# Layer-norm factors applied behind the projection, and ScalarE shares a multiplication with GpSimd, in a Fourier-attention block followed by a recurrent layer

## The chip, the core and the metric

One core of one Trainium2 chip runs the kernel. The core has five engines with their own instruction queues: TensorE (PE in the profile; its weight loads are PEld), VectorE (DVE), ScalarE (ACT), GpSimd (POOL) and SyncE (SP), which here only issues DMAs. They meet through semaphores. The metric is the device time of one launch in microseconds (us).

## The reference, cut to what matters

The input is `x`, 4 x 32 tokens of 128 x 128 float32. A Fourier attention block with a mixer is added to it; the result `t`, seen as rows of 128 values, goes through a second layer norm, a projection `W`, a batch norm and a sigmoid recurrence with `V`.

```python
x = x + conv_ref(ln_c(x), ...)            # attention, mixer, instance norms
t = to_tokens(x)                          # rows of 128 values
t = t + ffn_ref(ln_t(t), W, V, gamma, beta)

def ln_t(v, eps=1e-5):                    # the second LayerNorm
    m = mean(v, -1); s = var(v, -1)
    return (v - m) / sqrt(s + eps)

def ffn_ref(x, W, V, gamma, beta):
    Wx = einsum('bti,hi->bth', x, W)
    mean, var = moments of Wx over all rows, one pair per h
    Wx = (Wx - mean) * rsqrt(var + 1e-5) * gamma + beta
    # y_t = sigmoid(Wx_t + y_(t-1) @ V.T), scanned over t
```

The last step of the mixer in `conv_ref` adds, for every token, a multiple `bet` of the mixer's first output to the attention's result and to the second Fourier product.

## The kernel before, in words

All data stay in three SBUF buffers of 128 x 16384 float32: BIG1, BIG2 and BIG3. Tokens are handled in groups of four (G4 = 32 groups, counted by g) and in chunks of sixteen tokens (XC = 8 chunks, counted by c; a chunk is four groups). The order of the work on each engine is written out by hand: each engine has a loop over steps `i`, and fixed lags say which group a part of the step works on. Waits on semaphores tie the loops of the engines together.

The stage that the change touches is the last loop before the recurrence. Its parts, by engine:

- GpSimd (L612 to L623): for each step `bm1`, m1 of group i times `bet` (L618, in place in BIG1, 512 columns), then `xm`, a0 of group i-1 plus that product (L623). Ahead of steps 7, 11, 15, ... it waits until the layer-norm factors of chunk (i-3)//4 - 1 are there (`ln2_coef`, L615), so its work comes in bursts of four steps. Behind the loop it adds `g0` to the 32 groups of a0 (L632), 24 of them (G0_EARLY) before it waits for the recurrence's first state.
- TensorE (L893 to L913): `pair` multiplies the second Fourier product for two groups into banks 4 to 7; then it transposes four tokens of the normalised m1 of group i-7 (L906), and multiplies the transposed group i-9 by `w_t` (L913) into bank 2 or 3.
- VectorE (L1468 to L1490): adds the Fourier product to a0 of group i-1 (`x1`, L1474), takes the row statistics of its four tokens (four bn_stats, recorded at L1193), at every fourth group works out the chunk's moments (L1202 to L1206, the last of which asks for a root), normalises the fourth token of every other group (L1483), takes statistics of W's product of group i-12 for the batch norm (L1488), and at steps 5, 9, 13, ... turns the root into the factors `ln_r` and `ln_b` (L1212, L1213, which increments `ln2_coef`).
- ScalarE (L1110 to L1131): the root (L977), the normalisation of four or three tokens of group i-6 from a0 into m1, with scale and bias per row (L1118), the copy of the transposed group from PSUM to `ln_w` (`move_lnw`, recorded at L390, "SML<-PS"), and the copy of W's product from PSUM to BIG3 (L1130).

When the batch norm's statistics are complete (`bn`), VectorE aggregates them (L1495), asks for one more root (L1175) and computes the factors; TensorE meanwhile runs WARM = 4 dummy matmuls of 512 columns (L919) and then the recurrence, 24 steps in four groups, on TensorE, VectorE (L1505) and ScalarE (L1139 to L1152). Results are transposed back and added to a0 (L1548), stored by SyncE, and a judge (L1529 to L1539) decides whether the recurrence has converged.

Helpers record many operations under one line: matmuls at L644, transposes at L648, copies at L390, bn_stats at L1193.

## Time and profile before

| what | us |
|---|---|
| median of three runs | 474.27 |
| lowest, highest | 474.26, 479.56 |
| the profiled execution, its own time | 473.51 |
| its span in the trace | 471.4 |
| PE busy | 361.6 |
| DVE busy | 345.7 |
| ACT busy | 263.7 |
| POOL busy | 234.0 |

The span is the stretch from the first to the last recorded instruction of the profiled execution; the 2.1 us between it and the execution's own time lie outside the trace. A busy time is a sum over the whole span, so it does not say which engine limits a stage. Stretches are given in us from the span's start.

### The profile page before, as it was taken

What the parts mean: (1) busy time and instruction counts of PE and PEld (TensorE: products, weight loads), DVE (VectorE), ACT (ScalarE), POOL (GpSimd) and SP (SyncE); (2) the same over time, 40 slices, a digit from 0 to 9 for tenths busy, and PEclk for the clock granted to TensorE, in tenths of its full rate; (3) what the DMA queues carried; (4) which work ended last, traced back from release to release, by engine and by line L of the source; (5) the groups of instructions that cost most, each with busy time, mean ns of one, the idle gap of its engine ahead of it and who ended that gap; (6) DMA issues with size and microseconds to landing.
All of it is one profiled execution on the core that took longest, in us unless ns stands there. A gap on an engine that the chain in (4) does not pass through costs nothing.

```text
span 471.4 us, 7104 instructions
## 1 busy us (share of the span) xinstructions
PE 361.6 (77%) x2409; PEld 279.3 (59%) x2409; DVE 345.7 (73%) x946; ACT 263.7 (56%) x530; POOL 234.0 (50%) x276
## 2 busy tenths in 40 slices
PE   0169999998948998899961956867777488999970
PEld 0169986884528998788861843433334135766970
DVE  3698512888969573999948477777778837899992
ACT  0778762620135874556511305989888797899200
POOL 1399960000027957999210567777666985300000
PEclk9979999999997999999995885998898979999995
DMA  8999896789140002999977000000000000000698
GB/s 214 264 295 309 234 296 180 163 233 424 81 179 2 1 1 24 118 129 143 126 93 87 2 0 0 3 0 0 0 1 1 0 0 1 0 3 0 188 287 243
DMA packets 60696, 50.97 MB, mean 108 GB/s; under 512 B 4513, under 2 KB 54097, under 8 KB 59633
## 3 DMA queue, kind: packets, MB, share of 16 engines
q1 hardware_dynamic: 40928, 41.79, 30.4%
q0 software_dynamic: 16512, 8.39, 14.6%
q10 hardware_dynamic: 3216, 0.30, 0.6%
q8 instruction: 21, 0.34, 0.3%
q14 instruction: 19, 0.15, 0.1%
HBM read 30.45 MB, written 16.88 MB: 100 GB/s over the span
## 4 chain that ended last, share of the span: by engine, by line
PE 34%; DVE 29%; POOL 19%; ACT 6%; issue 5%; ACTq 3%; DMA 1%; SPq 0%; POOLq 0%; DVEq 0%
PE PS L644 31%; POOL BIG L583 8%; DVE BIG L1300 4%; DVE SML L1193 4%; DVE BIG L1474 3%; POOL BIG L623 3%; DVE BIG L1548 2%; POOL BIG L618 2%; PE PS L648 2%; DVE SML L1488 2%; POOL BIG L602 2%; ACTq L1000 2%; ACT BIG L1118 2%; ACT SML L390 2%; DMA BIG<-xn_rows 1%
## 5 line engine op out<-in xcount | busy, mean ns | idle before, releaser
L644 PE MATMUL PS<-CST,BIG 128*128 128x128 f32 (+6 forms) x994 | 129.5, 324 | 22.5 <-ACT BIG L1014 9.4
L644 PEld LDWEIGHTS PS<-CST,BIG 128*128 128x128 f32 (+1 forms) x994 | 114.4, 202 | 41.9 <-issue 11.9
L648 PE MATMUL PS<-CST,BIG 128*128 128x128 f32 (+1 forms) x326 | 54.6, 314 | 47.7 <-ACT SML L390 22.8
L648 PEld LDWEIGHTS PS<-CST,BIG 128*128 128x128 f32 (+1 forms) x326 | 43.9, 194 | 71.8 <-issue 52.3
L596 POOL COPY BIG<-BIG 128x512 f32<-128x512 f32 x24 | 30.5, 1328 | 74.4 <-DMA BIG<-xn_rows 71.3
L1193 DVE BATCH_NORM_STATS2 SML<-BIG 128x6 f32<-128x128 f32 x256 | 53.4, 279 | 6.3 <-DMA BIG<-in_x 5.0
L618 POOL TENSOR_TENSOR BIG<-BIG,SML 128x512 f32<-128x512 f32 x32 | 33.2, 1038 | 45.9 <-DVE SML L1213 28.0
L644 PE MATMUL PS<-BIG 128*128 128x128 f32 (+2 forms) x450 | 53.5, 368 | 2.6 <-DVE BIG L1300 2.1
L390 ACT ACTIVATE BIG<-PS 128x512 f32<-128x512 f32 (+3 forms) x59 | 33.2, 572 | 33.5 <-PE PS L644 26.5
L644 PE MATMUL PS<-BIG,SML 128*128 128x256 f32 (+4 forms) x230 | 48.9, 415 | 0.0
L644 PEld LDWEIGHTS PS<-BIG 128*128 128x128 f32 (+2 forms) x450 | 40.6, 168 | 13.1 <-issue 8.2
L1118 ACT ACTIVATE BIG<-BIG,SML 128x128 f32<-128x128 f32 x112 | 46.0, 482 | 3.8 <-DVE SML L1213 3.8
L1505 DVE SCALAR_TENSOR_TENSOR PS<-BIG,SML,PS 128x256 f32<-128x256 f32 x92 | 41.2, 489 | 3.6 <-PE PS L644 3.5
L602 POOL TENSOR_TENSOR BIG<-BIG,SML 128x512 f32<-128x512 f32 x32 | 39.5, 2476 | 7.0 <-ACT BIG L1083 7.0
L644 PE MATMUL PS<-SML 128*128 128x512 f32 (+2 forms) x74 | 41.1, 640 | 0.6 <-ACT BIG L1130 0.6
L623 POOL TENSOR_TENSOR BIG<-BIG 128x512 f32<-128x512 f32 x32 | 40.5, 1267 | 0.0
L644 PEld LDWEIGHTS PS<-BIG,SML 128*128 128x128 f32 (+1 forms) x230 | 31.1, 178 | 15.2 <-ACT BIG L1152 3.5
L583 POOL TENSOR_SCALAR BIG<-BIG,SML 128x128 f32<-128x128 f32 x84 | 36.8, 446 | 0.0
L1152 ACT ACTIVATE BIG<-PS,SML 128x256 f32<-128x256 f32 x80 | 35.5, 474 | 0.4
L632 POOL TENSOR_TENSOR BIG<-BIG,SML 128x512 f32<-128x512 f32 x32 | 32.0, 1037 | 6.9 <-ACT BIG L1139 6.9
L1474 DVE TENSOR_TENSOR BIG<-BIG,PS 128x512 f32<-128x512 f32 x32 | 21.7, 678 | 18.5 <-POOL BIG L623 16.9
L390 ACT ACTIVATE SML<-PS 128x512 f32<-128x512 f32 x32 | 34.4, 1075 | 0.0
(209 smaller groups left out, 516.0 us busy)
## 6 DMA issues: line engine op xcount, KB each, us to landing
xn_rows<-BIG SPq DMA_DIRECT2D x8, 1024.0 KB, 7.7
BIG<-xn_rows SPq DMA_DIRECT2D x8, 1024.0 KB, 9.3
BIG<-in_x POOLq DMA_DIRECT2D x8, 1024.0 KB, 11.0
out_x<-BIG SPq DMA_DIRECT2D x32, 256.0 KB, 3.6
BIG<-wy_rows SPq DMA_DIRECT2D x16, 192.0 KB, 5.4
BIG<-BIG SPq DMA_DIRECT2D x16, 192.0 KB, 4.0
BIG<-in_L_conv_mixer_w SPq DMA_DIRECT2D x2, 544.0 KB, 7.4
CST<-in_const SPq DMA_DIRECT2D x1, 547.5 KB, 8.7
```

Source lines behind the costliest of these rows:

```text
L390: return e.activation(o, i, ACT.Copy) if e is scalar_engine else e.tensor_copy(o, i)
L583: last = pool.tensor_scalar(x_h[:, n, :], x_h[:, n, :], ln_r[:, n:n + 1], ln_b[:, n:n + 1], ALU.mult, ALU.add)
L602: pool.tensor_tensor(m1[:, v, :], a0[:, v, :], kap[:, v].unsqueeze(2).to_broadcast([128, 4, W]), ALU.mult).then_inc(S("ka0"), 1)
L618: pool.tensor_tensor(m1[:, v, :], m1[:, v, :], bet[:, v].unsqueeze(2).to_broadcast([128, 4, W]), ALU.mult).then_inc(S("bm1"), 1)
L623: pool.tensor_tensor(a0[:, v, :], a0[:, v, :], m1[:, v, :], ALU.add).then_inc(S("xm"), 1)
L644: return pe.matmul(o, l, rhs, start=start, stop=stop, **k)
L648: return pe.matmul(o, i, ident[0:n, 0:n], is_transpose=True, start=True, stop=True)
L1118: last = act.activation(m1[:, n, :], a0[:, n, :], ACT.Identity, scale=ln_r[:, n:n + 1], bias=ln_b[:, n:n + 1])
L1152: act.activation(at(y_s, g, i * 2 + (j0 + dj)), sums(g, dj), ACT.Sigmoid, bias=s("bb")).then_inc(S("state"), 1)
L1193: last = dve.bn_stats(ln_st[:, c % 2, row, :], src[:, XR * c + row, :])
L1474: TT(v, v, halves(4 + g % 4), ALU.add).then_inc(S("x1"), 1)
L1505: STT(sums(b, dj), wx_step[:, b, :, bass.ds(j, 1), :], s("bs"), sums(b, dj), ALU.mult, ALU.add).then_inc(S("vy_wx"), 1)
```

## The change

Three things are changed, and constants with them.

First, the layer norm is no longer applied ahead of the transposes. The row mean of W is taken off W at the start (`w_centred`, on VectorE), so a row's own mean drops out of the product. TensorE transposes a0 itself and multiplies by the centred W. The factor 1/sqrt(var+eps) of each row is then multiplied into W's product: VectorE reads the product from PSUM and the factors from SBUF, writes BIG3 and sums the result in the same instruction (`STT ... accum_out`, in place of bn_stats). ScalarE squares the result with an offset and sums that (`Square`, with an accumulator output), in place of the copy. The row factors lie one per partition, and are wanted along the free dimension in all partitions: SyncE writes the 128 x 16 factors of a chunk to DRAM (8 KB), waits, and reads them back broadcast to 128 partitions (1 MB) into the chunk's part of BIG1.

Second, GpSimd multiplies two of each four tokens by `bet`, and ScalarE the two others (`bm1_act`, two copies of 128 columns with a scale per row), six groups ahead.

Third, GpSimd's bursts are released by the chunk's moments (`root_of`) and not by its factors; the transposed group is copied to `ln_w` in another order of its columns; the last four products have banks of their own; and 11 of the `g0` additions, not 24, come before the wait for the first state, behind all moments.

```diff
-LAG_LN, LAG_TR, LAG_MV, LAG_W, LAG_WX, LAG_BN = 6, 7, 8, 9, 10, 12
+LAG_TR, LAG_MV, LAG_W, LAG_WX, LAG_SQ = 6, 7, 8, 9, 10
-G0_EARLY, WARM = 24, 4
+G0_EARLY, WARM = 11, 4
+BM_ACT, LEAD = 2, 6
+ROOTS_1 = XC + 6
...
+        row_scale = BIG1[:, :].rearrange("d (c h t) -> d c h t", c=XC, t=XR)
+        def w_bank(g):
+            return 2 + g % 2 if g < G4 - 4 else 8 - G4 + g
+        def scale_of(g):
+            return row_scale[:, g // 4, :, 4 * (g % 4):4 * (g % 4) + 4]
...
-            return copy(e, ln_w[:, n % 2].rearrange("w (h t) -> w t h", t=4),
-                        bank(n % 2).rearrange("w (t h) -> w t h", t=4))
+            return copy(e, ln_w[:, n % 2].rearrange("w (h t) -> w h t", t=4),
+                        bank(n % 2).rearrange("w (t h) -> w h t", t=4))
... SyncE
+            for c in range(XC):
+                sp.wait_ge(S("ln2_coef"), c + 1)
+                sp.dma_start(rs_rows[c], ln_r[:, XR * c:XR * c + XR]).then_inc(S("rs_out"), 16)
+                sp.wait_ge(S("rs_out"), 16 * (c + 1))
+                sp.dma_start(row_scale[:, c].rearrange("d h t -> d (h t)"),
+                             flat(rs_rows[c]).to_broadcast([128, H * XR])).then_inc(S("rs_in"), 16)
... GpSimd
-                    pool.wait_ge(S("ln2_coef"), (i - 3) // 4)
+                    pool.wait_ge(S("root_of"), ROOTS_1 + (i - 3) // 4)
                 if i < G4:
-                    v = slice(4 * i, 4 * i + 4)
+                    v = slice(4 * i + BM_ACT, 4 * i + 4)
...
+                    pool.wait_ge(S("bm1_act"), i)
...
+            pool.wait_ge(S("root_of"), ROOTS_1 + XC)
             for g in range(G4):
-                pool.wait_ge(S("ln2_act"), g + 1)
-                pool.wait_ge(S("ln2_dve"), LN2_DVE[g])
+                pool.wait_ge(S("lnw_filled"), g + 1)
... TensorE
+            pe.wait_ge(S("w_centred"), 1)
...
+                    pe.wait_ge(S("x1"), 2 * (g // 2) + 2)
-                        last = tr(PS[:, g % 2, 128 * j:128 * j + 128], m1[:, 4 * g + j, :])
+                        last = tr(PS[:, g % 2, 128 * j:128 * j + 128], a0[:, 4 * g + j, :])
...
-                    mm(bank(2 + g % 2), w_t, ln_w[:, g % 2]).then_inc(S("wx_filled"), 1)
+                    mm(bank(w_bank(g)), w_t, ln_w[:, g % 2]).then_inc(S("wx_filled"), 1)
... ScalarE
+            def bm1_act(g):
+                for n in range(4 * g, 4 * g + BM_ACT):
+                    last = act.activation(m1[:, n, :], m1[:, n, :], ACT.Copy, scale=bet[:, n:n + 1])
+                last.then_inc(S("bm1_act"), 1)
             empty(act, "zt2", 0, 8, move_zt(4))
+            act.wait_ge(S("ka0"), G4)
+            act.wait_ge(S("bet"), 1)
+            for g in range(LEAD):
+                bm1_act(g)
             empty(act, "ta2", 0, 8, move_ta(ta2, 0))
-            for i in range(G4 + LAG_WX):
+            for i in range(G4 + LAG_SQ):
...
-                    for n in range(4 * g, 4 * g + LN2_ACT[g % 2]):
-                        last = act.activation(m1[:, n, :], a0[:, n, :], ACT.Identity,
-                                              scale=ln_r[:, n:n + 1], bias=ln_b[:, n:n + 1])
...
+                if i + LEAD < G4:
+                    bm1_act(i + LEAD)
+                g = i - LAG_SQ
                 if g >= 0:
-                    act.wait_ge(S("wx_filled"), g + 1)
-                    act.activation(wx(g), bank(2 + g % 2).rearrange("d (h t) -> d h t", t=4),
-                                   ACT.Copy).then_inc(S("wx"), 1)
+                    act.wait_ge(S("pivot"), 1)
+                    act.wait_ge(S("wx"), g + 1)
+                    act.activation(scale_of(g), wx(g), ACT.Square, bias=s("npiv"),
+                                   accum_out=bn_sq[:, g:g + 1]).then_inc(S("bn"), 1)
... VectorE
+            dve.wait_ge(S("ffn_in"), 16 * 4)
+            link(dve.tensor_reduce(s("wm"), w_t, AX.X, ALU.add))
+            link(TS(s("wm"), s("wm"), 1.0 / W, None, ALU.mult))
+            TS(w_t, w_t, s("wm"), None, ALU.subtract).then_inc(S("w_centred"), 1)
...
-                if 0 <= g < G4 and LN2_ACT[g % 2] < 4:
-                    for n in range(4 * g + LN2_ACT[g % 2], 4 * g + 4):
-                        last = TS(m1[:, n, :], a0[:, n, :], ln_r[:, n:n + 1], ln_b[:, n:n + 1], ALU.mult, ALU.add)
...
+                    dve.reciprocal(rs, rs).then_inc(S("ln2_coef"), 1)
+                g = i - LAG_WX
                 if g >= 0:
-                    dve.wait_ge(S("wx"), g + 1)
-                    dve.bn_stats(bn_st[:, g, :], wx(g)).then_inc(S("bn"), 1)
-                if i % 4 == 1 and 0 <= i // 4 - 1 < XC:
-                    ln_coefs(i // 4 - 1, "ln2_coef")
+                    dve.wait_ge(S("wx_filled"), g + 1)
+                    if g % 4 == 0:
+                        dve.wait_ge(S("rs_in"), 16 * (g // 4 + 1))
+                    STT(wx(g), bank(w_bank(g)).rearrange("d (h t) -> d h t", t=4), 1.0, scale_of(g),
+                        ALU.mult, ALU.mult, accum_out=bn_sum[:, g:g + 1]).then_inc(S("wx"), 1)
...
-            link(dve.bn_aggr(sc[:, 60:62], bn_st.rearrange("d g c -> d (g c)")))
+            dve.tensor_reduce(sc[:, 60:61], bn_sum, AX.X, ALU.add)
+            link(dve.tensor_reduce(sc[:, 61:62], bn_sq, AX.X, ALU.add))
+            # four small operations turn the sums into mean and variance
```

## Rows read from the trace of the kernel before

**Rows 1.** The chain that ended last, shares of the span, from the page.
```profile
PE 34%; DVE 29%; POOL 19%; ACT 6%; issue 5%; ACTq 3%; DMA 1%; SPq 0%; POOLq 0%; DVEq 0%
```
**Rows 2.** A stretch: from:to, length, busy PE PEld DVE ACT POOL, PEclk, DMA, GB/s.
```profile
274.80:391.10 116.30, 77.77 (x312) 39.82 (x308) 87.22 (x258) 91.12 (x184) 84.93 (x79) 0.84 0.00 1
```
**Rows 3.** Timeline of POOL, 334 to 348: start, duration, line, idle before, releaser.
```profile
334.22 1.04 POOL L618 TENSOR_TENSOR BIG<-BIG,SML 128x512 f32<-128x512 f32 x1 [4.08 <-DVE SML L1213]
335.22 1.27 POOL L623 TENSOR_TENSOR BIG<-BIG 128x512 f32<-128x512 f32 x1
...
347.24 1.04 POOL L618 TENSOR_TENSOR BIG<-BIG,SML 128x512 f32<-128x512 f32 x1 [4.08 <-DVE SML L1213]
```
**Rows 4.** Timeline of DVE in the same stretch.
```profile
338.74 0.69 DVE L1474 TENSOR_TENSOR BIG<-BIG,PS 128x512 f32<-128x512 f32 x1 [2.38 <-POOL BIG L623]
...
343.15 0.22 DVE L1202 TENSOR_TENSOR SML<-SML 128x32 f32<-128x32 f32 x1
...
343.78 0.68 DVE L1488 BATCH_NORM_STATS2 SML<-BIG 128x6 f32<-128x512 f32 x1
344.38 0.67 DVE L1474 TENSOR_TENSOR BIG<-BIG,PS 128x512 f32<-128x512 f32 x1
345.08 0.87 DVE L1193 BATCH_NORM_STATS2 SML<-BIG 128x6 f32<-128x128 f32 x4
345.87 0.33 DVE L1483 TENSOR_SCALAR BIG<-BIG,SML 128x128 f32<-128x128 f32 x1
...
346.99 0.17 DVE L1213 SCALAR_TENSOR_TENSOR SML<-SML 128x16 f32<-128x16 f32 x1
```
**Rows 5.** Groups by line and shape, whole span: busy, mean ns, idle before.
```profile
L1083 ACT ACTIVATE BIG<-PS 128x512 f32<-128x512 f32 x32 | 18.7, 595 | 9.0 <-PE PS L644 8.6
L1051 ACT ACTIVATION_READ_ACCUMULATOR BIG<-BIG 128x1 f32 x1 | 0.2, 187 | 0.0
L1447 DVE SCALAR_TENSOR_TENSOR BIG<-BIG,SML 128x512 f32<-128x512 f32 x2 | 2.2, 1158 | 0.0
```
**Rows 6.** Timeline of ACT: four normalisations in one piece.
```profile
334.18 1.65 ACT L1118 ACTIVATE BIG<-BIG,SML 128x128 f32<-128x128 f32 x4 [0.47 <-DVE SML L1213]
```
**Rows 7.** DMA issues: KB each, us from issue to landing.
```profile
BIG<-in_x POOLq DMA_DIRECT2D x8, 1024.0 KB, 11.0
BIG<-in_L_conv_mixer_w SPq DMA_DIRECT2D x2, 544.0 KB, 7.4
wy_rows<-BIG SPq DMA_DIRECT2D x1, 96.0 KB, 6.2
BIG<-in_L_conv_key_w ACTq DMA_DIRECT2D x1, 18.0 KB, 2.5
```
**Rows 8.** Timeline of PE: product and pair at half clock, transposes and product at full.
```profile
292.24 1.92 PE L644 MATMUL PS<-SML 128*128 128x512 f32 x2
294.09 2.08 PE L644 MATMUL PS<-CST,BIG 64*128 64x256 f32 x8
...
341.12 0.63 PE L648 MATMUL PS<-CST,BIG 128*128 128x128 f32 x4
341.58 1.02 PE L644 MATMUL PS<-SML 128*128 128x512 f32 x2
```
**Rows 9.** Timelines, end of the loop: DVE in the last moments and at the last root.
```profile
368.74 1.07 DVE L1203 TENSOR_TENSOR SML<-SML 128x16 f32<-128x16 f32 x1
392.14 0.15 DVE L1175 TENSOR_SCALAR SML<-SML 128x1 f32<-128x1 f32 x1
```
**Rows 10.** Timeline of PE: the recurrence's first products.
```profile
394.86 12.71 PE L644 MATMUL PS<-BIG,SML 128*128 128x256 f32 x56
```
**Rows 11.** Stretches around an idle TensorE; columns as in rows 2.
```profile
250.00:254.00 4.00, 0.00 (x0) 0.00 (x0) 3.68 (x12) 0.00 (x0) 0.00 (x0) 0.50 1.26 158
258.00:262.00 4.00, 4.00 (x20) 3.31 (x20) 2.48 (x9) 1.18 (x2) 0.00 (x0) 0.50 0.00 0
262.50:264.50 2.00, 1.70 (x16) 1.43 (x14) 1.25 (x4) 1.02 (x2) 0.22 (x1) 1.00 0.00 0
```

More of the change, by code:

```diff
@@ L311, in metaformer @@
         ln_tmp = SML[:, 2496:2624].rearrange("p (k v) -> p k v", v=16)
-        bn_st = SML[:, 1984:2176].rearrange("p (g c) -> p g c", c=6)
+        bn_sum = SML[:, 1984:1984 + G4]
+        bn_sq = SML[:, 2016:2016 + G4]
         scn = {}
@@ L334, in metaformer @@
         wy_rows = nc.dram_tensor("wy_rows", [NH, 3 * MW * MH], F32).ap()
+        rs_rows = nc.dram_tensor("rs_rows", [XC, H, XR], F32).ap()
         xn_tok = nc.dram_tensor("xn_rows", [NT, H, W], F32).ap()
@@ L350, in metaformer @@
         modes_ps = PS[:, 4:6, :].rearrange("t a n -> t (a n)")
-        LN2_DVE = np.cumsum([LN2_ACT[g % 2] < 4 for g in range(G4)]).tolist()
         P2_N = [min(P2_T, NT - P2_T * g) for g in range((NT + P2_T - 1) // P2_T)]
@@ L1465, in _ @@
             empty(dve, "ta2", 0, 8, move_ta(ta2, 0))
-            for i in range(G4 + LAG_BN):
+            assert roots[0] == ROOTS_1
+            for i in range(G4 + LAG_WX):
                 g = i - 1
@@ L1479, in _ @@
                         ln_rows(g // 4, a0, four_at(g % 4))
-                g = i - LAG_LN
-                if 0 <= g < G4 and LN2_ACT[g % 2] < 4:
-                    for n in range(4 * g + LN2_ACT[g % 2], 4 * g + 4):
-                        last = TS(m1[:, n, :], a0[:, n, :], ln_r[:, n:n + 1], ln_b[:, n:n + 1], ALU.mult, ALU.add)
-                    last.then_inc(S("ln2_dve"), 1)
-                g = i - LAG_BN
-                if g >= 0:
-                    dve.wait_ge(S("wx"), g + 1)
-                    dve.bn_stats(bn_st[:, g, :], wx(g)).then_inc(S("bn"), 1)
-                if i % 4 == 1 and 0 <= i // 4 - 1 < XC:
-                    ln_coefs(i // 4 - 1, "ln2_coef")
+                if i % 4 == 1 and 0 <= i // 4 - 1 < XC:
+                    c = i // 4 - 1
+                    roots[0] += 1
+                    dve.wait_ge(S("root"), roots[0])
+                    rs = ln_r[:, XR * c:XR * c + XR]
+                    dve.reciprocal(rs, rs).then_inc(S("ln2_coef"), 1)
+                g = i - LAG_WX
+                if g >= 0:
+                    dve.wait_ge(S("wx_filled"), g + 1)
[3 more added lines that the diff above has]
+                        ALU.mult, ALU.mult, accum_out=bn_sum[:, g:g + 1]).then_inc(S("wx"), 1)
+                    if g == 0:
+                        dve.wait_ge(S("wx"), 1)
+                        TS(s("npiv"), bn_sum[:, 0:1], -1.0 / (4 * H), None, ALU.mult).then_inc(S("pivot"), 1)
             dve.memset(start_b[:, 0, 0:NT:TB], 0.0)
             dve.wait_ge(S("bn"), G4)
-            link(dve.bn_aggr(sc[:, 60:62], bn_st.rearrange("d g c -> d (g c)")))
+            dve.tensor_reduce(sc[:, 60:61], bn_sum, AX.X, ALU.add)
+            link(dve.tensor_reduce(sc[:, 61:62], bn_sq, AX.X, ALU.add))
+            link(TS(sc[:, 60:61], sc[:, 60:61], 1.0 / (NT * H), None, ALU.mult))
+            link(TT(s("x0"), sc[:, 60:61], s("npiv"), ALU.add))
+            link(TT(s("x0"), s("x0"), s("x0"), ALU.mult))
+            link(STT(sc[:, 61:62], sc[:, 61:62], 1.0 / (NT * H), s("x0"), ALU.mult, ALU.subtract))
             inv_root(s("bs"), sc[:, 61:62], EPS, s("gamma"))
```

16 lines of the change are left out of this document (5 added, 11 removed).

## The prediction

> **What bounds the kernel now.** I read the chain of waits first. TensorE, VectorE and GpSimd share it [rows 1], so no engine bounds the whole kernel and a stage has to be read by itself. Then the busy times of the stage that the change rewrites, from the first addition of the second Fourier product to the complete batch-norm sums, 274.8 to 391.1 us: in 116.3 us no engine is busy for more than 91, DMA is idle, and the mean granted clock is 0.84 [rows 2]. So a loop of waits sets the pace, and the timelines show it. GpSimd starts a burst of four steps at 334.22 and the next at 347.24, 13.02 us apart, and stood idle for 4.08 us ahead of each, released by L1213, the layer-norm factors on VectorE [rows 3]. VectorE stood idle for 2.38 us until the burst's second addition, worked to the chunk's moments at 343.15 (done by 343.78), and reached L1213 at 346.99 only behind a statistics pass, an addition, four row statistics and a normalisation that its loop puts in between [rows 4]. GpSimd 4.5, VectorE 5.0, then 3.4 between moments and factors: that is the 13.0. At the end of the loop the last moments meet GpSimd's g0 additions, and an operation with two small SBUF inputs takes 1.07 us [rows 9] where its group of four took 0.63 [rows 4].
>
> **The change part by part.** All sums are against the profiled execution (span 471.4, time 473.5; the median shown is 0.8 above that).
>
> *GpSimd.* Its burst is released by the moments, 3.4 us earlier, and L618 covers half the columns: by its 1.04 us about 0.55, against 1.27 for the addition [rows 3]. Less the overlap of neighbours a burst takes 4 x (0.55 + 1.23) = 7.1 us, its half that VectorE wants first 3.6. VectorE now has a longer way to its next moments than that, so GpSimd leaves the path.
>
> *VectorE.* Per step it keeps the addition, 0.70 start to start, and four row statistics, 0.79 [rows 4]. It loses the statistics pass (0.60) and half a normalisation, and gets a product of 512 columns from PSUM and SBUF with a sum. The trace has no such form. The nearest rows are L1488, 0.60 start to start over the same view [rows 4], and, on the dear side, L1447, an operation of the same kind with both tensors in SBUF, 1.16 [rows 5]; reading out the sum costs 0 to 0.19, ScalarE's price for it [rows 5]. Its one SBUF tensor and PSUM tensor are as in L1474, which runs undisturbed, so I take 0.75, ends 0.60 and 1.35. A step is then 0.70 + 0.79 + 0.75 = 2.24. Four make 9.0; with moments 0.75 and the reciprocal 0.25 a chunk takes 10.0.
>
> The Trainium skill (Vector Engine (DVE) Microarchitecture Reference, Points that are easy to get wrong) says that this kind with two SBUF sources that aren't bf16 runs at half speed. The 1.16 us of L1447 agrees. By that rule one source in PSUM escapes it; were the rule to hold for it too, the sum would be that of the first rival below.
>
> *ScalarE.* Per step it loses 3.5 normalisations and a copy. It keeps the move to `ln_w`, now in the order of columns that L1083 has: 0.60 [rows 5]. It gets two copies of 128 columns, 1.65 / 4 = 0.41 each [rows 6], so 0.82, and a square of 512 columns with a sum: 0.60 as L1083, and 0.19 to read out [rows 5]. That is 2.2, with the root some 9.1 a chunk, under VectorE but close. For two engines that hand work to each other at 90% I add 0.2: 10.2 us a chunk.
>
> *TensorE* does the same work. At full clock a group's transposes take 0.46 to the next start and a product about 0.87, a pair half of 2.08: 4 x 1.33 + 2 x 1.04 = 7.4 us a chunk; at half clock 14.9 [rows 8]. Under 10.2, so it idles little.
>
> *SyncE and the DMA.* The path from factors to broadcast is a new wait: store 8 KB, wait, load 1 MB. The small store I take at 2.5, the load of 18 KB, with 6.2 (96 KB to DRAM under load) as upper end. For the load of 1 MB I take 5.5, between 2.5 and 7.4 (544 KB broadcast, beside other traffic), upper end 11.0 [rows 7]. With 0.3 for the two starts L = 8.3, between 5.3 and 17.5. No other transfer runs then. VectorE waits for it four steps behind the factors, 10.2 us, so in the loop it is hidden, until L passes 10.2; then two chunks take L + 10 us. At the last chunk nothing covers it.
>
> The Trainium skill (DMA: Bandwidth & Descriptors, Anatomy of one DMA and Specifications) gives about 2.0 us plus bytes over 436 GB/s, an estimate of 2.0 and 4.4 for the two; it also says that pieces under 512 B are read, changed and written, which speaks against the 64 B pieces of this store. No row here has that store, and by the first rule the end would come 1.6 us earlier than I say.
>
> *The start.* ScalarE does the first 12 half-multiplications ahead of its moves of `ta2`: 4.9 us, of which most hides behind TensorE filling the other banks. I charge 0.7. Centring W adds three small operations to VectorE early, while it waits for other engines: nothing, and at most 0.8 if that cover were gone. Squares and sums in place of bn_stats change the end by 0.2.
>
> *The clock.* At the end TensorE finishes its products about 8 us before the sums are complete. In the rows, an idle TensorE is at 0.50, the lower level, 1.2 GHz (250 to 254); still at 0.50 through four busy microseconds (258 to 262), and at 1.00, 2.4 GHz, from 262.5 [rows 11]. So the dummy matmuls start low. Eight halves of 0.92 at the low level [rows 8]: 4.5 us low, the rest at full, 6.2 in all with the small matmul ahead, against 3.8 now. The recurrence starts 2.4 later after the sums. A low clock at the first products costs me 1.0 more.
>
> *The sum.* First addition 275.5. Four steps of 1.49 and moments: 282.2. The next step and factors of chunk 0: 284.0. Steps 6 to 8 wait for GpSimd (3.6 us behind 282.2) and meet its burst in the moments; factors of chunk 1 at 291.9; the row factors of chunk 0 land at 284.0 + 8.3 = 292.3. From there 0.75 + 3 x 2.24 + 0.75 + 1.5 + 0.3: factors of chunk 2 at 302.3. Four chunks of 10.2: 343.1. The last has no further addition: 343.1 + 10.2 - 1.5 = 351.8. Landing 8.3 later, 360.1. Four products 3.0, the last square 0.8: 363.9. Small operations 1.2: root asked at 365.1, against 392.14 [rows 9]. The recurrence starts at 363.9 + 6.2 = 370.1 against 394.86 [rows 10]. That is 24.8 earlier, less 1.0 for the clock at the start: 23.8. GpSimd's 21 remaining g0 additions take 22 us of a recurrence of 44, hidden. 473.5 - 23.8 = 449.7; against the median 450.5. I predict 450.
>
> **The rivals.**
> 1. *Dear operations.* If the product with its sum takes 1.16 to 1.2, a chunk is 12.0 and the six chunks and the tail give back 1.8 x 6 = 11: 461. For it: L1447 [rows 5]. Against: L1474 and L1488, both 0.6 to 0.7 with this view or a PSUM source.
> 2. *The transfer paces the loop.* At L = 12 two chunks take 22 and not 20.4, three times, and the tail is 3.7 longer: 450 + 5 + 4 = 459. For it: 7.4 us for half the bytes, broadcast [rows 7]. Against: that one ran beside others.
> 3. *The transfer makes it slower.* The same mechanism, further out: the end moves 4 us for each 1 us of L beyond 10.2 (three pairs of chunks and the tail). To eat up 24 us it takes L = 16, to be slower by 2% 18. With 6.2 + 11.0, the dearest rows of either kind [rows 7], L is 17.5: 450 + 2 + 4 x 7.3 = 481. Against: both rows were taken with the DMA engines full, and here they are empty [rows 2].
> 4. *TensorE at half clock.* If it falls as it does now in this stage (0.84 on average), products take twice as long for some microseconds. All of the loop at 14.9 a chunk would give 450 + 28 = 478, no change. For it: 0.50 after idle stretches [rows 11]. Against: at 7.4 of 10.2 busy and with busy stretches that bring the clock back, only pieces of it.
> 5. *Cheap operations.* Product 0.60, L 6.7: 0.7 x 6 + 1.6: 444.
> 6. *The change doesn't do what it says*: the release at the moments brings nothing because additions wait for ScalarE's halves. They are six groups ahead, so I give it nothing of its own; it is part of 4.
>
> **How the numbers follow.** Forecast 0.55, rivals 0.15, 0.13, 0.04, 0.06, 0.07. Two per cent of 474.27 is 9.5, about what a measurement of this kernel tells from no change: faster is under 464.8. The forecast, 1, 5 and nearly all of 2 lie there: 0.89. Rival 4 and the edge of 2 give 0.07 within 2%, rival 3 gives 0.04. The range 442 to 464 holds the forecast (446 to 455), most of 1, 2 and 5, and leaves out 3 and 4.
>
> **What would show it.** GpSimd's bursts 10 to 10.5 us apart, released by L1206's successor and not by the factors, and no idle VectorE ahead of the addition. The product's row near 0.7 us; a read-out row behind it or none. `ln_w` moves of 0.6. VectorE idle for 5 to 6 us once, ahead of product 28, released by the broadcast. TensorE at 0.50 when the dummy matmuls start. Wrong would be: bursts over 12 us apart, an idle VectorE at every fourth product (the transfer), or TensorE over 90% busy in the loop.

## The result and the profile after

The changed kernel takes 438.99 us (median of four runs, 437.13 to 440.65) against 474.34 us before on the same chip: a ratio of 0.9229, 95% interval 0.9188 to 0.9269. The forecast was 450 with 442 to 464: the direction was right, and the gain, 35 us where 24 were forecast, was larger than the range allowed.

| | before | after |
|---|---|---|
| profiled execution, its own time | 473.51 | 440.65 |
| its span | 471.4 | 438.7 |
| first addition of the loop | 274.81 | 277.37 |
| moments of the eighth chunk done | 371.78 | 347.31 |
| root of the batch norm asked | 392.14 | 359.01 |
| recurrence starts | 394.86 | 361.71 |

From first addition to root the stage went from 117.3 to 81.6 us. Of that, 27.0 lies between the first addition and the last moments (the loop), and 8.7 behind them, where ScalarE used to pace the last groups: before the change VectorE's statistics waited up to 2.23 us for its copies there.

```profile
383.12 0.69 DVE L1488 BATCH_NORM_STATS2 SML<-BIG 128x6 f32<-128x512 f32 x1 [2.23 <-ACT BIG L1130]
```

The stage after the change in one row, to be held against [rows 2] (same columns):

```profile
277.30:357.90 80.60, 65.51 (x312) 35.85 (x309) 73.40 (x266) 56.09 (x149) 58.01 (x63) 0.96 0.30 106
319.00:349.00 30.00, 24.55 (x117) 12.99 (x116) 28.85 (x107) 20.94 (x53) 19.15 (x21) 1.00 0.29 107
```

In the middle of the loop (second row) VectorE is busy for 28.85 of 30 us. Before, no engine was the bound, the waits between them were; now one is, at 96%. TensorE runs at 1.00 there, and the DMA engines, idle before, are busy for 29%.

GpSimd's timeline, as [rows 3]:

```profile
319.56 0.61 POOL L635 TENSOR_TENSOR BIG<-BIG,SML 128x256 f32<-128x256 f32 x1 [2.02 <-DVE SML L1232]
320.13 1.28 POOL L642 TENSOR_TENSOR BIG<-BIG 128x512 f32<-128x512 f32 x1
...
328.83 0.61 POOL L635 TENSOR_TENSOR BIG<-BIG,SML 128x256 f32<-128x256 f32 x1 [2.01 <-DVE SML L1232]
```

The bursts are 9.27 us apart (13.02 before), released by the moments. VectorE over one of its steps and over the moments, as [rows 4]; L1505 is the addition, L1219 the row statistics, L1522 the product:

```profile
304.38 0.87 DVE L1219 BATCH_NORM_STATS2 SML<-BIG 128x6 f32<-128x128 f32 x4
305.17 0.67 DVE L1522 SCALAR_TENSOR_TENSOR BIG<-PS,BIG 128x512 f32<-128x512 f32 x1
305.77 0.08 DVE L1522 DVE_READ_ACCUMULATOR BIG<-PS,BIG 128x1 f32 x1
305.77 0.68 DVE L1505 TENSOR_TENSOR BIG<-BIG,PS 128x512 f32<-128x512 f32 x1
306.48 0.87 DVE L1219 BATCH_NORM_STATS2 SML<-BIG 128x6 f32<-128x128 f32 x4
...
309.49 0.21 DVE L1228 TENSOR_TENSOR SML<-SML 128x32 f32<-128x32 f32 x1
...
310.12 0.68 DVE L1522 SCALAR_TENSOR_TENSOR BIG<-PS,BIG 128x512 f32<-128x512 f32 x1
...
312.24 0.23 DVE L1516 RECIPROCAL SML<-SML 128x16 f32<-128x16 f32 x1
312.39 0.62 DVE L1522 SCALAR_TENSOR_TENSOR BIG<-PS,BIG 128x512 f32<-128x512 f32 x1
```

From start to start the product takes 0.60, the addition 0.71 and the statistics 0.79: 2.10 a step. (The operation behind the addition reads what it wrote, the one behind the product does not; whether that is the 0.11 between them was not tested.) The read-out of the sum has a row of its own, 0.08 us, that starts at the same moment as the next addition. With moments and reciprocal a chunk takes 9.28 us, and from 289 to 348 us no row shows VectorE idle. ScalarE over one step:

```profile
319.73 0.58 ACT L400 ACTIVATE SML<-PS 128x512 f32<-128x512 f32 x1
320.21 0.68 ACT L1129 ACTIVATE BIG<-BIG,SML 128x128 f32<-128x128 f32 x2
320.79 0.71 ACT L1156 ACTIVATE BIG<-BIG,SML 128x512 f32<-128x512 f32 x1
321.40 0.19 ACT L1156 ACTIVATION_READ_ACCUMULATOR BIG<-BIG,SML 128x1 f32 x1
321.50 0.58 ACT L400 ACTIVATE SML<-PS 128x512 f32<-128x512 f32 x1
```

The step takes 1.77 us; 2.2 were forecast. The new transfer, from the page's DMA issues, and the end of the loop on VectorE and TensorE:

```profile
BIG<-rs_rows SPq DMA_DIRECT2D x8, 1024.0 KB, 4.6
```
```profile
350.50 0.69 DVE L1522 SCALAR_TENSOR_TENSOR BIG<-PS,BIG 128x512 f32<-128x512 f32 x1 [0.60 <-PE PS L663]
...
354.17 0.69 DVE L1522 SCALAR_TENSOR_TENSOR BIG<-PS,BIG 128x512 f32<-128x512 f32 x1 [1.67 <-DMA BIG<-rs_rows]
...
359.01 0.15 DVE L1201 TENSOR_SCALAR SML<-SML 128x1 f32<-128x1 f32 x1
```
```profile
357.95 3.92 PE L663 MATMUL PS<-CST,SML 128*128 128x1 f32 x10 [1.78 <-ACT BIG L1156]
```

Behind the last moments VectorE is no longer full: its products come 1.30 us apart, each waiting for TensorE's product, which waits for ScalarE's copy. SyncE issues the store at 348.12 and the load at 349.52, and it lands at 354.17: 6.08 us from the factors (348.09), of which VectorE stood idle for 1.67. TensorE had been idle for 1.78 us when the dummy matmuls began, and they ran at full clock, 3.9 us.

### The profile page after: what moved, and what is told of

It reads as the page before. It is cut to its first block, busy times and chain, and to the rows that moved or that the text cites. A ratio compares the mean times of both kernels' runs of the same rounds, so it can differ in the third digit from the quotient of the medians.

```text
span 438.7 us, 7163 instructions
## 1 busy us (share of the span) xinstructions
PE 352.2 (80%) x2409; PEld 278.3 (63%) x2409; DVE 332.1 (76%) x963; ACT 233.8 (53%) x514; POOL 220.5 (50%) x276
## 4 chain that ended last, share of the span: by engine, by line
PE 37%; DVE 30%; POOL 15%; issue 8%; ACT 4%; ACTq 3%; DMA 2%; SPq 0%; DVEq 0%; POOLq 0%
PE PS L663 34%; POOL BIG L600 8%; DVE BIG L1330 5%; DVE SML L1219 4%; DVE BIG L1505 4%; DVE BIG L1522 3%; PE PS L667 3%; DVE BIG L1589 3%; POOL BIG L619 2%; ACTq L1020 2%; DMA BIG<-xn_rows 2%; DVE BIG L1422 1%; DVE BIG L1418 1%; POOL BIG L642 1%; POOL BIG L635 1%
## 5 line engine op out<-in xcount | busy, mean ns | idle before, releaser
L663 PE MATMUL PS<-CST,BIG 128*128 128x128 f32 (+6 forms) x994 | 127.2, 318 | 21.1 <-ACT BIG L1034 8.0
L667 PE MATMUL PS<-CST,BIG 128*128 128x128 f32 (+1 forms) x326 | 51.0, 300 | 15.2 <-DVE BIG L1477 14.3
L663 PE MATMUL PS<-BIG 128*128 128x128 f32 (+2 forms) x450 | 55.8, 375 | 2.6 <-DVE BIG L1330 2.1
L1219 DVE BATCH_NORM_STATS2 SML<-BIG 128x6 f32<-128x128 f32 x256 | 53.4, 279 | 5.8 <-DMA BIG<-in_x 4.5
L663 PEld LDWEIGHTS PS<-BIG 128*128 128x128 f32 (+2 forms) x450 | 42.8, 175 | 13.2 <-issue 8.4
L619 POOL TENSOR_TENSOR BIG<-BIG,SML 128x512 f32<-128x512 f32 x32 | 39.5, 2476 | 7.0 <-ACT BIG L1103 7.0
L663 PE MATMUL PS<-SML 128*128 128x512 f32 (+2 forms) x74 | 35.2, 560 | 9.3 <-DVE BIG L1522 8.0
L651 POOL TENSOR_TENSOR BIG<-BIG,SML 128x512 f32<-128x512 f32 x32 | 32.0, 1042 | 9.3 <-issue 6.3
L635 POOL TENSOR_TENSOR BIG<-BIG,SML 128x256 f32<-128x256 f32 x32 | 19.6, 612 | 33.8 <-DVE SML L1490 17.5
L663 PE MATMUL PS<-SML,BIG 128*128 128x128 f32 (+1 forms) x264 | 33.1, 287 | 1.0 <-DVE SML L1376 1.0
L663 PEld LDWEIGHTS PS<-SML,BIG 128*128 128x128 f32 (+1 forms) x264 | 32.1, 202 | 2.0 <-DVE SML L1376 1.3
L1113 ACT ACTIVATE BIG<-BIG,SML 128x512 f32<-128x512 f32 x32 | 22.8, 721 | 19.0 <-DVE BIG L1418 19.0
```

Of the source, the lines that this page charges most:

```text
L619: pool.tensor_tensor(m1[:, v, :], a0[:, v, :], kap[:, v].unsqueeze(2).to_broadcast([128, 4, W]), ALU.mult).then_inc(S("ka0"), 1)
L635: pool.tensor_tensor(m1[:, v, :], m1[:, v, :], bet[:, v].unsqueeze(2).to_broadcast([128, 4 - BM_ACT, W]), ALU.mult).then_inc(S("bm1"), 1)
L651: pool.tensor_tensor(a0[:, v, :], a0[:, v, :], g0[:, v].unsqueeze(2).to_broadcast([128, 4, W]), ALU.add).then_inc(S("x1_g0"), 1)
L663: return pe.matmul(o, l, rhs, start=start, stop=stop, **k)
L667: return pe.matmul(o, i, ident[0:n, 0:n], is_transpose=True, start=True, stop=True)
L1219: last = dve.bn_stats(ln_st[:, c % 2, row, :], src[:, XR * c + row, :])
```

## The experiments

In all of them "chunk" is the distance between the moments of neighbouring chunks in the profiled execution. The runs were made in three sets, each with the kernel before in it; its medians there were 474.9, 475.6 and 476.5 us, and each ratio is against its own set.

**1. After, with GpSimd released by the factors again.**

```diff
-                    pool.wait_ge(S("root_of"), ROOTS_1 + (i - 3) // 4)
+                    pool.wait_ge(S("ln2_coef"), (i - 3) // 4)
```

> The changed kernel, with GpSimd's bursts again released by the chunk's factors and not by its moments. Theory A (in the new loop VectorE's own work, 9.28 us a chunk, is the pace, and the early release only keeps GpSimd out of its way): the factors come 2.3 us behind the moments, the half of the burst that VectorE wants first takes 3.65 more, and VectorE wants it 4.85 behind the moments, so it waits 1.1 us a chunk: chunks of 10.4 us, 6 to 8 us in all, some 446. Rival B (the release was the whole gain, the rest only moved work about): chunks go back to about 13 us, some 460. Rival C (the release is worth nothing once the operations are cheaper): 439.

447.47 us, ratio 0.9452 (0.9367 to 0.9536); chunks of 10.47 us.

```profile
317.56 0.69 DVE L1505 TENSOR_TENSOR BIG<-BIG,PS 128x512 f32<-128x512 f32 x1 [1.10 <-POOL BIG L642]
```

VectorE's wait for GpSimd is back, 1.10 us once a chunk (the next is at 328.03, 10.47 later). The release is worth 1.2 us a chunk here, 8.5 in all by the medians. Not all of that is the wait: the ten dummy matmuls took 5.62 us and not 3.92, for the granted clock fell within a microsecond or so of their start (0.71 in 364 to 365, 0.50 in 365 to 367). That is theory A; B (460) and C (439) are out.

**2. Before, with only the release at the moments.**

```diff
-                    pool.wait_ge(S("ln2_coef"), (i - 3) // 4)
+                    pool.wait_ge(S("root_of"), XC + 6 + (i - 3) // 4)
```

> The kernel before, with nothing changed but that GpSimd's bursts are released by the moments. Theory A: the loop of 13.02 us was GpSimd 4.5, VectorE 5.0 and 3.4 between moments and factors; without the 3.4 the next limit is ScalarE, which idles 1.64 us of the 13.02, so chunks of 11.4 and a total 8 to 11 us shorter than before, some 464 to 466. Rival B (the release is the whole gain): chunks near 9.6, 445. Rival C (it is worth nothing without cheaper operations): 474.

463.41 us, ratio 0.9739 (0.9687 to 0.979); the first two chunks behind the first moments take 9.6, then 10.74, one of them 11.96.

```profile
328.00:350.00 22.00, 16.01 (x80) 8.17 (x78) 21.31 (x68) 22.00 (x47) 17.95 (x16) 1.00 0.01 1
```
```profile
360.90 1.07 DVE L1203 TENSOR_TENSOR SML<-SML 128x16 f32<-128x16 f32 x1
```

The first row is a stretch of two chunks, the columns those of [rows 2]: ScalarE is busy for all 22 us. The one line frees 11 us, and then ScalarE's normalisations and copies are the bound. The last chunk takes 13.60, because its moments meet the `g0` additions, as in [rows 9] (second row).

**3. After, with all four multiplications on GpSimd.** `BM_ACT = 0`; ScalarE's halves and the wait for them are taken out.

```diff
-BM_ACT, LEAD = 2, 6
+BM_ACT, LEAD = 0, 6
```

> The changed kernel without ScalarE's halves: GpSimd multiplies all four tokens again. Theory A: the first half of a burst takes 4.6 us, VectorE wants it at 4.85, so that does not wait; but the burst now ends 9.3 us behind the moments that released it, and the next moments start at 8.5, so one of the small operations with two SBUF inputs waits 0.6 to 0.8 us for the end of GpSimd's instruction: chunks of about 10.0 and 3 to 6 us more in all, 442 to 445. Rival B (GpSimd had slack all along): 439 or, with the work taken from ScalarE, less. Rival C (GpSimd becomes the pace, each small operation waits): chunks of 11 or more, over 449.

442.82 us, ratio 0.9358 (0.9277 to 0.944); chunks of 9.60.

```profile
318.77 0.54 DVE L1215 TENSOR_TENSOR SML<-SML 128x32 f32<-128x32 f32 x1
...
319.72 0.68 DVE L1509 SCALAR_TENSOR_TENSOR BIG<-PS,BIG 128x512 f32<-128x512 f32 x1
```
```profile
319.88 1.04 POOL L635 TENSOR_TENSOR BIG<-BIG,SML 128x512 f32<-128x512 f32 x1 [0.64 <-DVE SML L1219]
```

GpSimd's burst (9.0 us) ends just as the moments begin: their first operation takes 0.54 instead of 0.22, and GpSimd idles for only 0.64 us before it is released. The halves are worth 0.3 us a chunk in the finished kernel, not the 1.8 us that they take off GpSimd's burst. The larger part of the 3.8 us lies in the first two chunks, which take 1.7 and 0.7 us more than with the halves (9.58 and 9.61, not 7.88 and 8.86): VectorE waits for the first burst there, 1.49 us and not 0.65.

**4. After, without the throttle on GpSimd.** Its wait for the moments is taken out; it then runs as far ahead as ScalarE's halves let it.

```diff
-                if i >= 7 and i % 4 == 3:
-                    pool.wait_ge(S("root_of"), ROOTS_1 + (i - 3) // 4)
```

> The changed kernel, with GpSimd's waits for the moments taken out, so that it runs through its 32 groups in one piece, about 60 us long, to some 326 us of the span. Theory A (VectorE's small operations with two SBUF inputs wait for the end of GpSimd's instruction): the four of each chunk's moments take 3 to 4 us in place of 0.63 for the chunks up to then, five of the eight: 12 to 16 us more, 451 to 455. Rival B (the wait is only there for order, nothing meets): 439 or less.

445.57 us, ratio 0.9407 (0.9325 to 0.9489).

```profile
281.60 4.38 DVE L1225 TENSOR_TENSOR SML<-SML 128x32 f32<-128x32 f32 x1
...
292.93 1.30 DVE L1226 TENSOR_TENSOR SML<-SML 128x16 f32<-128x16 f32 x1
```
```profile
281.71 0.60 POOL L632 TENSOR_TENSOR BIG<-BIG,SML 128x256 f32<-128x256 f32 x1
282.29 1.25 POOL L639 TENSOR_TENSOR BIG<-BIG 128x512 f32<-128x512 f32 x1
...
285.30 0.60 POOL L632 TENSOR_TENSOR BIG<-BIG,SML 128x256 f32<-128x256 f32 x1
287.53 1.26 POOL L639 TENSOR_TENSOR BIG<-BIG 128x512 f32<-128x512 f32 x1 [1.63 <-ACT BIG L1126]
```

Right in kind, too dear in size. An operation of VectorE with two small SBUF inputs, 0.2 us of work, took 4.38 us while GpSimd issued one operation straight behind another, and ended only when GpSimd itself had to wait for ScalarE. Only the first was so dear, with 4.2 us; the next five chunks lost 2.2 us together (four of them took 9.4 to 9.8), and the last two took 9.28. Why the first operation waited through several of GpSimd's and the later ones through one at most (1.30 shown), the traces don't show. So the wait that the change moves, but keeps, is worth 6.6 us; it is not a mere leftover.

**5. After, with 24 early `g0` additions.** `G0_EARLY = 24`.

> The changed kernel with 24 of the g0 additions ahead of the wait for the first state, as before the change, and not 11. GpSimd then works until 25 us behind the last moments and not 11, over the batch norm's small operations. Theory A (an operation of VectorE with two SBUF inputs waits until GpSimd stops reading SBUF, and in the unthrottled run one of them waited 4.4 us through several instructions): six such operations lie between the sums and the recurrence, each waits for up to 1 us or more: 3 to 8 us more, 442 to 447. Rival B (nothing meets, the recurrence's start hangs on TensorE's dummy matmuls): 439.

442.0 us, ratio 0.9329 (0.9251 to 0.9406). The loop is unchanged; from first addition to root it takes 84.17 us and not 81.64.

```profile
357.02 0.96 DVE L1535 TENSOR_TENSOR SML<-SML 128x1 f32<-128x1 f32 x1
358.02 0.96 DVE L1536 SCALAR_TENSOR_TENSOR SML<-SML 128x1 f32<-128x1 f32 x1
359.01 0.15 DVE L1201 TENSOR_SCALAR SML<-SML 128x1 f32<-128x1 f32 x1
```

Three of the small operations ahead of the root take one `g0` addition each (0.96 instead of 0.16); L1201, which has one tensor input, does not. Two more do so behind the root, so the recurrence starts 88.0 us behind the first addition and not 84.3. This is why the change lowered that constant: 3.7 us of its 35 by the profiles, 3.0 by the medians.

**6. After, with the transfer 2.8 us later:** the store of the factors is made three times, each waited for.

```diff
-                sp.dma_start(rs_rows[c], ln_r[:, XR * c:XR * c + XR]).then_inc(S("rs_out"), 16)
-                sp.wait_ge(S("rs_out"), 16 * (c + 1))
+                for k in range(LATE):
+                    sp.dma_start(rs_rows[c], ln_r[:, XR * c:XR * c + XR]).then_inc(S("rs_out"), 16)
+                    sp.wait_ge(S("rs_out"), 16 * (LATE * c + k + 1))
```

> The changed kernel, with each chunk's 8 KB store done three times in a row, so that the broadcast lands 2.8 us later: 8.9 us behind the factors and not 6.1. VectorE wants it 9.1 behind them. Theory A (in the loop it stays hidden, the tail pays): 2.8 us more at the last chunk alone; TensorE idles 4.6 us and not 1.8 there, and if its clock falls for that the start of the recurrence pays 2 more: 442 to 444. Rival B (the transfer paces the loop already, or disturbs it): several us more a chunk, over 450.

447.29 us, ratio 0.9415 (0.9382 to 0.9449): 3 us over the expected end.

```profile
320.44 3.13 SPq L536 DMA_DIRECT2D rs_rows<-SML  x3
326.14 0.32 SPq L538 DMA_DIRECT2D BIG<-rs_rows  x1
```
```profile
330.80 0.69 DVE L1524 SCALAR_TENSOR_TENSOR BIG<-PS,BIG 128x512 f32<-128x512 f32 x1 [1.11 <-DMA BIG<-rs_rows]
```
```profile
360.95 7.17 PE L665 MATMUL PS<-CST,SML 128*128 128x1 f32 x10 [4.03 <-ACT BIG L1158]
367.96 4.25 PE L665 MATMUL PS<-BIG,SML 128*128 128x256 f32 x18
```
```profile
360.00:364.00 4.00, 3.05 (x5) 1.60 (x6) 1.86 (x12) 2.67 (x7) 0.00 (x0) 0.59 0.00 0
```

By the medians the kernel is 8.3 us over the plain one; from the first addition on, the profile is 9.0 us longer, and that comes from three places. In the loop VectorE waited for the transfer twice, 2.6 us more in all: once where three stores took 5.7 us and not the usual 4.2 (both shown), and once at the first chunk, whose landing was as early as the others (9.05 us behind its factors) but is wanted 7.8 behind them and not 9.2. The tail, from the last moments to the root, took 14.8 and not 11.7, as the transfer landed 9.2 us behind the factors and not 6.1; VectorE's wait grew from 1.67 to 3.93. And TensorE, idle for 4.03 us and not 1.78 ahead of the dummy matmuls, ran them at the lower clock (0.50 from 361 to 367; 0.59 is the mean of the row): 7.17 us and not 3.92, 3.2 more. The last is the clock term of the prediction, seen in a kernel in which the tail is as late as the prediction had supposed.

**7. After, with the transfer 7 us later:** as 6, with six stores.

> The same with the store done six times: the broadcast lands 7.1 us later, 13.2 behind the factors. Theory A (two chunks then take the transfer and one chunk's work): 13.2 + 9.3 = 22.5 for two chunks where they take 18.6 now, three and a half times, 12 to 14 us; 7.1 at the tail, and some 2 for TensorE's clock: 21 to 24 in all, 460 to 463. Rival B (only the tail pays): 446 to 449.

474.06 us over ten runs, ratio 0.9973 (0.995 to 0.9997): the whole gain is gone.

```profile
309.98 0.69 DVE L1524 SCALAR_TENSOR_TENSOR BIG<-PS,BIG 128x512 f32<-128x512 f32 x1 [4.61 <-DMA BIG<-rs_rows]
321.83 0.69 DVE L1524 SCALAR_TENSOR_TENSOR BIG<-PS,BIG 128x512 f32<-128x512 f32 x1 [2.42 <-DMA BIG<-rs_rows]
333.89 0.69 DVE L1524 SCALAR_TENSOR_TENSOR BIG<-PS,BIG 128x512 f32<-128x512 f32 x1 [2.63 <-DMA BIG<-rs_rows]
```
```profile
388.22 6.84 PE L665 MATMUL PS<-CST,SML 128*128 128x1 f32 x10 [7.42 <-ACT BIG L1158]
394.90 5.33 PE L665 MATMUL PS<-BIG,SML 128*128 128x256 f32 x23
```

My expectation put the delay at 7 us and was 11 to 14 too low. From the first issue to the last, six stores took 7.35 us at the first chunk, with no load beside them, and 8.4 to 11.5 at the others, all begun within 2.4 us of the issue of the load of the chunk before. So L, from factors to landing, was 13.3 us at the first chunk, 19.7 at the second and 14.5 to 17.0 from the third on. The prediction's own formula then holds: two chunks take L and a chunk's own work, 14.5 + 9.3 = 23.8, and the chunks whose moments end at 328.99 and 341.05 took 11.85 + 12.06 = 23.9; 16.5 + 9.3 = 25.8 against 14.04 + 11.85 = 25.9; the other pairs agree to 0.5. TensorE idles beside VectorE, and its mean granted clock is 0.56 to 0.58 over the eight microseconds behind the longer waits (295 to 303, 311 to 319, 349 to 357).

**8. After, with neither the halves nor the release:** the edits of 1 and 3 together, so that only the factors have moved.

> The changed kernel without ScalarE's halves and with the release by the factors: what is left is the layer norm's factors behind the product. Theory A (VectorE 9.28 a chunk, plus what it waits for GpSimd): half a burst of 4.6 us, released 2.3 behind the moments, is there at 6.9 where VectorE wants it at 4.85, 2.05 us a chunk; the burst's end meets the moments for 0.5 to 0.8 more: chunks of 11.9 to 12.1, 455 to 460. Rival B (the effects of the two parts add, 8.5 and 3.8 as measured one by one): 451.

455.0 us, ratio 0.9571 (0.9536 to 0.9606); chunks of 11.85.

```profile
330.60 1.04 POOL L635 TENSOR_TENSOR BIG<-BIG,SML 128x512 f32<-128x512 f32 x1 [2.91 <-DVE SML L1503]
```

That is theory A, at its lower edge; B, with 451, is out. With this the parts stand against each other (the times are from different sets, whose kernel before lay between 474.3 and 476.5):

| kernel | chunk | time |
|---|---|---|
| before | 13.02 | 474.3 |
| release alone (2) | 10.74 | 463.4 |
| factors alone (8) | 11.85 | 455.0 |
| factors and halves (1) | 10.47 | 447.5 |
| factors and release (3) | 9.60 | 442.8 |
| all three | 9.28 | 439.0 |

By chunks the release gives 2.3 alone, and 2.25 (8 to 3) beside the factors; the halves give 1.4 without the release and 0.3 with it. The factors give only 1.2 a chunk alone, and yet some 20 us in all: the last chunk no longer meets the `g0` additions (10.3 us, not 14.9), and from the last moments to the root it takes 11.9 us and not 20.4, without the normalisations in ScalarE's queue.

**9. After, without the sums** (no accumulator output on VectorE and ScalarE; the batch norm's sums are constants, so its statistics are left out).

```diff
-                        ALU.mult, ALU.mult, accum_out=bn_sum[:, g:g + 1]).then_inc(S("wx"), 1)
+                        ALU.mult, ALU.mult).then_inc(S("wx"), 1)
```

> The changed kernel, with both accumulator outputs taken away (VectorE's product and ScalarE's square give no sum; the batch norm's sums are then constants, so its statistics are left out). Theory A (the sum costs VectorE nothing at its pace: the read-out of 0.08 us lies beside the next addition, and the product would be 0.60 start to start without it too): chunks stay at 9.28 us, root asked within 0.3 of 359.0, 438 to 441. ScalarE loses its read-out of 0.19 a group and idles more, without effect. Theory B (the sum is in the 0.60): chunks 8.9 to 9.1 and 435 to 437. Rival C (ScalarE is in the path too, coupled with VectorE): chunks 9.0 to 9.1, with the product no shorter.

439.42 us, ratio 0.9253 (0.9217 to 0.9288), against 439.43 for the changed kernel in the same set; chunks of 9.22 or 9.23. A sum on VectorE costs 0.05 / 4 = 0.01 us of its pace: theory A. B and C, with chunks of 8.9 to 9.1, are out.

**10. After, with the copy to `ln_w` in its old order.** The columns lie in `ln_w` in the same order in both kernels; what differs is the order in which the copy goes through them. The changed kernel reads PSUM with a stride and writes without one, this one reads without and writes with one.

```diff
-            return copy(e, ln_w[:, n % 2].rearrange("w (h t) -> w h t", t=4),
-                        bank(n % 2).rearrange("w (t h) -> w h t", t=4))
+            return copy(e, ln_w[:, n % 2].rearrange("w (h t) -> w t h", t=4),
+                        bank(n % 2).rearrange("w (t h) -> w t h", t=4))
```

> The changed kernel with the columns of the transposed group in the order of before. Theory A: its copy on ScalarE goes from 0.60 back to 0.97 start to start, ScalarE's chunk is then 4 x (0.97 + 0.59 + 0.81) + 0.2 = 9.7 us against VectorE's 9.28 while it has multiplications of the mixer to do (to step 26), under it behind them; so three to five chunks of 9.7 and 440.5 to 442. TensorE's product that reads the contiguous columns is no shorter. Rival B (ScalarE has room for it, since its queue has idle time): chunks 9.28, 438.5 to 440.

443.38 us, ratio 0.9328 (0.9284 to 0.9371), 4 us over the unedited kernel of the same set. But the way there was neither A nor B.

```profile
349.90 1.11 ACT L400 ACTIVATE SML<-PS 128x512 f32<-128x512 f32 x1
350.78 0.70 ACT L1156 ACTIVATE BIG<-BIG,SML 128x512 f32<-128x512 f32 x1
```
```profile
354.16 1.13 PE L663 MATMUL PS<-SML 128*128 128x512 f32 x2 [0.41 <-ACT SML L400]
356.99 5.62 PE L663 MATMUL PS<-CST,SML 128*128 128x1 f32 x10 [1.70 <-ACT BIG L1156]
```

The chunks are 9.28, as B said: with 0.87 for the copy a ScalarE step is 2.13, and four are 8.5, under VectorE. The cost lies behind the loop. There VectorE no longer sets the pace, ScalarE does, with 1.55 us for copy and square; from first addition to root it takes 83.16 and not 81.63 us, and TensorE, kept waiting between the last products, does the dummy matmuls partly at the lower clock (0.98 in 357 to 358, 0.50 in 358 to 361), 5.62 and not 3.92. 1.5 + 1.7 = 3.2, which is what this profile has over that of experiment 11 from the first addition on.

**11. The unedited changed kernel again.**

> The changed kernel once more, unedited, for the chunks and for the scatter between its executions. Expected: chunks of 9.28 us, root asked 82 us behind the first addition. Its executions lie at two levels, near 437.3 and 440.5; if the upper one is TensorE at the half clock at 80 to 88 us, in code that the change does not touch, the profile of this run shows 0.50 there and a time near 440.5, or 0.9 to 1.0 there and a time near 437.5.

439.43 us, ratio 0.9264 (0.921 to 0.9318). The profiled execution took 438.72; its loop is the same to 0.02 us (chunks of 9.27 to 9.29, root 81.63 behind the first addition), and its first addition is at 275.58 and not 277.37. TensorE in code that the change does not touch, first in the profile shown above, then in this one:

```profile
84.00:86.00 2.00, 2.00 (x11) 2.00 (x11) 1.10 (x5) 1.07 (x4) 0.00 (x0) 0.50 0.00 0
```
```profile
84.00:86.00 2.00, 2.00 (x20) 2.00 (x20) 1.31 (x3) 0.80 (x5) 0.00 (x0) 1.00 0.24 49
```

The lower clock at 80 to 88 us was there in the slower execution and not in this one, as said; but this one was 1.2 above the level of 437.5 that I gave it, so the dip is at most a part of the scatter. No other profile here has that dip, and yet the first addition lies at 276.94 in experiment 12 and at 280.16 in experiment 2, where the clock is lower in other stretches (0.80 in 170 to 190, where this profile has 0.94); in all the others it lies between 273.98 and 275.77.

**12. After, with the last four products in the two old banks.** Their wait for the last additions becomes the wait for a free bank that the other products have (not in the cut).

```diff
-            return 2 + g % 2 if g < G4 - 4 else 8 - G4 + g
+            return 2 + g % 2
```

> The changed kernel with the last four products in the two old banks. Theory A (the four products wait in PSUM for the last factors' round trip): with two banks only two products can be ready, so products 30 and 31 are made one by one behind VectorE's reading of 28 and 29; product 0.24 at full clock, 1.0 us at half clock after an idle TensorE, so the end comes 0.3 to 1.5 us later, 439 to 441. TensorE's last product ends near 357 and not 356.2, which leaves it warmer: the dummy matmuls then cost the same or less. Rival B (no change): 437 to 440.5.

441.11 us, ratio 0.9292 (0.9255 to 0.933). The intervals of this and of 11 overlap, so the times alone decide nothing. In the profile the root is asked 82.41 us behind the first addition and not 81.63.

```profile
355.77 0.69 DVE L1520 SCALAR_TENSOR_TENSOR BIG<-PS,BIG 128x512 f32<-128x512 f32 x1 [0.67 <-PE PS L663]
```

VectorE waits for the third of the last products: the banks are worth 0.8 us, inside A's 0.3 to 1.5, by one profile of each.

## Why the prediction was right and wrong

**The mechanism was right.** The loop of waits [rows 3, 4] was the bound; released by the moments, GpSimd left the path (experiments 1, 2), and VectorE's own work set the pace. The shape of the sum held at each point: factors of chunk 1 16.34 us behind the first addition (16.4 forecast), GpSimd ahead of VectorE from then on, one wait for the transfer at the end and none before.

**The sizes were off, nearly all to one side.** The step that failed is the pricing of the new parts. The product with its sum (0.75, measured 0.60) and an addition for coupling (0.2, measured 0) made a chunk 10.2 us where it took 9.28; the transfer at the end was put at 8.3 and took 6.08; and 3.4 us were charged for a low clock that cost nothing. From the forecast for the profiled execution, 449.7, to what it did:

- *The product with its sum*, 0.75 forecast, was 0.60, the lower bound. The row whose pace it had is L1488, 0.60 over the same view [rows 4]; I chose the addition L1474 for its two sources, 0.70, and the rest for a read-out that costs 0.01 (experiment 9). Four times 0.15 a chunk.
- *The reciprocal*, 0.25, was 0.15 start to start, and *the coupling*, 0.2, was 0: VectorE has no idle row in the loop. ScalarE was at 70% and not near 90%, as its step is 1.77. Together with the product that is 0.92 us a chunk: 10.2 became 9.28. From chunk 1 to the last factors it makes 5.5 us.
- *The transfer*, L = 8.3, was 6.08: 1.4 for the store with the way to the next issue (2.5 taken from a load of 18 KB), 4.6 for the load (5.5 taken). 2.2 us at the last chunk. The Trainium skill (DMA: Bandwidth & Descriptors, Anatomy of one DMA) gave 6.4 in all as an estimate. The page has that formula for transfers issued by GpSimd, which the prediction leaves out; these two are issued by SyncE. Its fixed part is more than the store took, its 4.4 for the load close to the measured 4.6. Of the price that its section Specifications puts on short pieces, the 64 B pieces of this store show nothing at this size.
- *The clock of the dummy matmuls*, 2.4 us: they took 3.92 and not 6.2. The prediction had TensorE done 8 us ahead of the sums; it was idle for only 1.78. The tail was 2.3 us shorter, and TensorE's last product ended 8.1 us behind the last factors and not 4, as it had to wait for ScalarE's copy of the last group. That the term itself is real is shown by experiments 6 (4.03 idle, 7.17), 1 and 10 (5.62).
- *The clock at the first products*, 1.0, and *the start*, 0.7, cost nothing. TensorE was at 0.50 in 284 to 288, but VectorE waited in that part only for GpSimd, 0.65 us. From the table `bet` to the first addition both kernels take 10.68 us; ScalarE's twelve halves took 3.61, 0.29 each and not the 0.41 of L1118 [rows 6].

With 0.2 for small terms these are 12.0 us. Two things went the other way: the early part was 2.6 us later in that execution, partly by the clock dip at 80 to 88 us (experiment 11), and 0.3 was lost behind the start of the recurrence. 449.7 - 12.0 + 2.6 + 0.3 = 440.6, against 440.65.

**Why the range missed.** The rival for this case, cheap operations, was at 444, and the range ended at 442. It moved two terms, the product to its lower end and L to 6.7, where the lower end was 5.3, and left the coupling, both clock charges and the start in the sum. Those were four additions, all of one sign, and none of them came. What should have been seen is that they could all be absent at once: a shorter step takes load off the pair of engines, and a shorter tail leaves TensorE idle for less (no guarantee of the full clock, as experiments 1 and 10 show). 444 less 1.2 (coupling over six chunks), 3.4 (the two clock charges) and 0.7 (the start) is 438.7: a range that took in the bounds of the unknown costs had to reach it. That it meets the measured time so closely is partly luck: the rest of L and of the reciprocal, some 1.2 us that it still has too much, and the later first addition go opposite ways.

**The rivals.** Dear operations: the product never took more than 0.69. By the Trainium skill (Vector Engine (DVE) Microarchitecture Reference, Points that are easy to get wrong) the half speed is for two SBUF sources; one source in PSUM and 0.60 start to start agree. The transfer as the bound, up to no gain: not here at L = 6.1, but experiment 7 shows that it is a real cliff, in the place and with the formula given; it gave back everything at L = 14.5 to 17.0, where the prediction said 16. That these agree is partly luck: the prediction had 24 us to lose and the edge at 10.2, and 35 went, from an edge at 9.2 (7.8 at the first chunk). TensorE at half clock: 0.50 in 284 to 288, 0.96 in 288 to 292 and 1.00 from there to the end of the loop. "The change doesn't do what it says" fell with experiment 1.

**What stays open.** Experiment 4's later chunks (9.4 to 9.8) were not taken apart, and its one wait of 4.38 us is seen but not explained. The 1.2 us by which the execution without a dip lies above the lower level are unexplained, as is the first addition of experiment 12. What makes the clock fall in the dummy matmuls is open too: the idle stretch ahead of them alone does not tell, see the last line below.

## What to carry to other kernels

When no engine is full, write down the cycle of waits, and ask for each wait whether its releaser is the earliest event that is enough: one changed line gave 11 us, before any work was moved. But a wait can also be a throttle that keeps GpSimd away from another engine's small operations; move it, and don't drop it. And add no term for interaction without a row that shows it, and where several such terms have one sign, let the range reach to where all of them are gone.
